# Maxima of a group set 0.13 of a head behind its turn instead of 0.07

## What is computed

```python
q = rmsnorm(x @ Wq); k = rmsnorm(x @ Wk); v = x @ Wv          # 16 heads of 64
gate = softplus(einsum('bthd,hd->bht', k, u_n) / sqrt(D))
bias = -dist[None, None] * omega_eff[None, :, None, None] * gate[:, :, None, :]
bias = where(causal[None, None], bias, -inf)
scores = einsum('bihd,bjhd->bhij', q, k) * scale + bias
attn = softmax(scores, axis=-1)
y = einsum('bhij,bjhd->bihd', attn, v).reshape(B, T, H * D)
```

## Time and profile before

| | us |
|---|---|
| median of 3 runs | 3415.65 (3412.11 to 3420.32) |
| profiled execution | 3416.66 |
| its span in the trace | 3414.9 |
| PE busy | 3174.5 (93%) |
| ACT busy | 1796.5 (53%) |
| DVE busy | 1667.0 (49%) |
| POOL busy | 1499.5 (44%) |
| L907 (PE, maxima), busy / idle before | 463.6 / 79.1 |

### The profile page before, as it was taken

The page is one execution under the profiler, slowest core; times in us unless marked ns, Lnnn a source line. Parts: engine busy times, 40 slices in busy tenths (PEclk is TensorE's granted clock), DMA queues, the critical chain, the costliest instruction groups (busy, mean ns, idle before and its releaser), DMA issues. The chain is left out here.

```text
span 3414.9 us, 45979 instructions
## 1 busy us (share of the span) xinstructions
PE 3174.5 (93%) x15472; PEld 2462.6 (72%) x15472; DVE 1667.0 (49%) x3920; ACT 1796.5 (53%) x3057; POOL 1499.5 (44%) x1318
## 2 busy tenths in 40 slices
PE   4999999999999999999999999779999999899998
PEld 3667767767667677677677676557777878688887
DVE  6566565566565665655655666242222222232322
ACT  1576676667666666666766677532222222222222
POOL 4576676666666666666765666411111110000000
PEclk7899999999999999999999999889999999899999
DMA  2232332322432422322323223343222321322120
GB/s 75 66 89 55 69 79 51 84 62 55 92 79 61 98 55 56 92 54 68 84 49 80 66 54 89 88 120 94 87 87 86 89 87 42 99 73 74 38 74 19
DMA packets 196539, 249.12 MB, mean 73 GB/s; under 512 B 67280, under 2 KB 95056, under 8 KB 196176
## 3 DMA queue, kind: packets, MB, share of 16 engines
q1 hardware_dynamic: 196304, 246.19, 28.1%
HBM read 84.86 MB, written 43.52 MB: 38 GB/s over the span
## 5 line engine op out<-in xcount | busy, mean ns | idle before, releaser
L385 POOL TENSOR_TENSOR e_lo<-e_all,e_hi 128x512 fp32r<-128x512 f32 (+1 forms) x832 | 1031.8, 1248 | 676.3 <-ACT e_all L627 618.3
L627 ACT ACTIVATE e_all<-ps_s,bias 128x512 f32<-128x512 f32 (+3 forms) x1280 | 790.6, 623 | 182.4 <-PE ps_s L929 73.1
L620 ACT ACTIVATE e_hi<-ps_s,bias 128x512 fp32r<-128x512 f32 (+1 forms) x832 | 559.5, 672 | 272.2 <-PE ps_s L927 173.3
L814 DVE TENSOR_REDUCE maxes<-ps_m 128x1 f32<-128x512 f32 x768 | 519.5, 686 | 340.6 <-PE ps_m L907 336.4
L907 PE MATMUL ps_m<-k_ext,q_max 128*128 128x512 f32 (+3 forms) x1280 | 463.6, 382 | 79.1 <-issue 30.1
L926 PE MATMUL ps_s<-q_twice,k_split 128*128 128x512 f32 (+3 forms) x1280 | 484.5, 378 | 6.1 <-ACT e_all L627 3.1
L927 PE MATMUL ps_s<-q_ext,k_ext 128*128 128x512 f32 (+3 forms) x1280 | 472.3, 369 | 0.0
L960 PE MATMUL ps_v<-e_lo,v_main 128*66 128x512 f32 (+1 forms) x832 | 432.9, 520 | 15.5 <-POOL e_lo L385 15.5
L811 DVE CUSTOM_DVE_ANT_0 ps_m<-ps_m,mask_row 128x128 f32<-128x128 f32 (+3 forms) x512 | 253.6, 497 | 363.9 <-PE ps_m L907 360.4
L907 PEld LDWEIGHTS ps_m<-k_ext,q_max 128*128 128x128 f32 x1280 | 246.9, 194 | 230.2 <-issue 81.5
L949 PE MATMUL ps_v<-e_hi,v_main 128*66 128x512 f32 (+1 forms) x832 | 324.8, 390 | 0.0
(11 more groups left out here) (247 smaller groups left out, 6120.5 us busy)
## 6 DMA issues: line engine op xcount, KB each, us to landing
q_twice<-q_max SPq DMA_DIRECT2D x256, 128.0 KB, 2.3
yt<-y_out SPq DMA_DIRECT2D x128, 130.0 KB
k_ext<-kq_hi SPq DMA_DIRECT2D x128, 128.0 KB, 2.3
q_max<-kq_hi SPq DMA_DIRECT2D x128, 128.0 KB, 2.4
k_split<-kq_hi SPq DMA_DIRECT2D x128, 128.0 KB, 2.4
k_split<-kq_lo SPq DMA_DIRECT2D x128, 128.0 KB, 2.4
q_ext<-kq_lo SPq DMA_DIRECT2D x128, 128.0 KB, 2.4
y_in<-yt SPq DMA_DIRECT2D x128, 128.0 KB, 3.0
```

The costliest lines, as they stand in the source:

```text
L385: on.tensor_tensor(e_lo[:, i % LO_RING, off:QB], e_all[:, u_ % E_RING, off:QB], e_hi[:, i % HI_RING, off:QB].bitcast(F32), ALU.subtract).t ...
L620: nc.scalar.activation(e_hi[:, i % HI_RING, off:QB], ps_s[u_ % 2][:, off:QB], ACT.Exp, bias=by).then_inc(hi_done, 1)
L627: nc.scalar.activation(e_all[:, u_ % E_RING, off:QB], ps_s[u_ % 2][:, off:QB], ACT.Exp, bias=by).then_inc(ex_done, 1)
L814: nc.vector.tensor_reduce(maxes[:, qt, kc:kc + 1], ps_m[m % 2][:, 0:width], AX.X, ALU.max).then_inc(mx_free, 1)
```

## The change

The distance at which maxima may stand behind their group's turn becomes 0.13 of a head instead of 0.07. The maxima of a pair's first head run from there to t0 + 0.24 (before: t0 + 0.20), those of the second from t0 + 0.27 (before: t0 + 0.24) to t0 + 1.08 as before.

```diff
--- before.py
+++ after.py
@@ -119,10 +119,10 @@
             turns = [first + 0.005 + 0.066 * i for i in range(NTURN)]
             for i, when in enumerate(turns):
                 at(when, "turn", n, i)
-            start, end = (turns[0] + 0.07, t0 + 0.20) if s == 0 else (t0 + 0.24, t0 + 1.08)
+            start, end = (turns[0] + 0.13, t0 + 0.24) if s == 0 else (t0 + 0.27, t0 + 1.08)
             for v, (qt, kc) in enumerate(MAXES):
                 qb = qt // TQ
-                when = max(start + (end - start) * v / (NM - 1), turns[qb] + 0.07)
+                when = max(start + (end - start) * v / (NM - 1), turns[qb] + 0.13)
                 at(when, "max", n, v)
                 if v + 1 == maxes_to(qb):
                     at(when + 0.001, "most", n, qb)
```

## The result

The changed kernel takes **3401.34 us** (median of 9 runs, 3397.03 to 3408.38) where the kernel before, on the same chip, takes 3415.65 (9 runs, 3412.11 to 3424.59): a ratio of 0.9959, 95% interval 0.9947 to 0.9971. That is faster by 14.3 us. The forecast was 3384 us, a gain of 31.5; the time lies inside the wide range (3350 to 3406), but outside the forecast's own (3370 to 3397), and more than half of the gain is missing. The profiled execution took 3401.34 us with a span of 3399.6, 15.3 us less than the one of before (3414.9), so the two traces show the whole difference.

A forecast was written before the change was run, and what follows sets the result against it. PE was taken as the bound in attention, with 84.7 us hanging on operand waits and lost clock. Terms 37.7 - 1.2 - 5 = 31.5 us gave 3384 us from 3415.65; own range 3370 to 3397, wide range 3350 to 3406.

The forecast's parts named there:

- The mechanism: First maxima wait less; ACT, before turn 3's copy into kq_hi, waits for turn 1's transfers, so PE stands 1.9 us at unit 24.
- The first rival: Turn 3's copy holds nobody up and the waits simply go: 68 us come back, 3348 us, chance 0.12.
- the fourth: Rival: the first maximum's release moves with PE's order and the stall returns in full; 3416 us, chance 0.07.
- The third: Rival: the clock falls for double length, 3.4 us, in every pair, 51 us in all; slower, 3430 us, chance 0.06.
- The second rival: The clock falls behind each new wait, 25.5 us in place of 5: a gain of 11, 3404 us, chance 0.15.
- left at the first maxima and second groups: First maxima of 15 pairs keep about 0.9 us each, 15 us in all; second groups no longer wait for q_max.
- new wait for e_all: Behind turn 3, unit 24's scores wait for e_all: 1.9 us in pair 1, about 33 us in all.
- clock still lost: Behind the new waits before unit 24, three clock falls at 1.7 us: -5 us (0 to 25).
- The step that failed first: DVE becoming the bound with maxima closer (0.81 of a head, not 0.84) was left out: busy 22.1 of 46 us.
- Unit 24: Starts 1.1 us behind the landing of turn 1's last transfer; mark to mark over 15 pairs a gain of 37.7 us.
- The first maximum: In each pair it comes 2.07 us later behind nine matmuls, the release stays at 202.1 (pair 1), about 0.9 us left.
- The start: Before the program's first scores, three maxima leave PE's idle wait for q_twice and DVE's chain comes later: -1.2 us (0.7 to 2).

The follow-up runs named there:

- the ring of three: The changed kernel with kq_hi and kq_lo as rings of three buffers in place of two (x_rows sharing sq's memory): 3361.47 us (0.9833).
- late loads: The changed kernel with the five w_in transfers issued 0.3 of a head later (t0 - 2.30 in place of t0 - 2.60): 3362.64 us (0.9841).
- the ring alone: The kernel before, distance 0.07, with kq_hi and kq_lo as rings of three buffers and x_rows in sq: 3414.76 us (0.9998).
- the shorter queue alone: The kernel before, distance 0.07, with the w_in transfers issued at t0 - 2.30 in place of t0 - 2.60: 3402.22 us (0.9957).
- with both: The changed kernel with kq_hi and kq_lo as rings of three buffers and the w_in transfers issued at t0 - 2.30: 3358.74 us (0.983).

## Why the mechanism was right and the sum was wrong

**The mechanism** was the one forecast. The first maximum no longer waits 2.9 us; turn 3's copy in ACT waits for turn 1's q_ext; unit 24 stands behind it; the second groups' first maxima wait in three places (1.8 us in all) where they waited 11.7. The first rival (nobody waits for turn 3) is refuted by the 42.7 us on ACT before turn 3's copy and by the ring of three, the fourth (nothing moves) by 1.09 in place of 2.91. The third (slower) did not come. The second rival has the nearest time, 3404, but with the clock falling behind each wait; it fell seven times. That its time comes nearest is luck. And that 3401 lies inside the range at all comes of a range drawn wide enough to take in that rival.

**The sum** failed in its sizes. In the terms of the forecast, with the trace's own numbers:

| | forecast | measured |
|---|---|---|
| left at the first maxima and second groups | 15 | 22.6 |
| new wait for e_all | 33 | 20.2 |
| more waits for DVE's maxima | 0 | 10.6 |
| more at e_lo and x_rows | 0 | 2.7 |
| clock still lost | 5 | 11.9 |

The first two together are 42.8 us, 5 below the forecast. The three others are 20 us above it; the net of 15 is nearly all of the 16.2 us that the traces lack of the forecast gain (15.3 in place of 31.5).

- **The step that failed first** is the one that left DVE out: "it is busy for 22.1 of 46 us there". The row is right, but it is a mean, and it begins 16 us behind the second head's turn 0, while the largest new wait stands 3 us behind that turn. Cutting the trace of before at the same marks gives 22.6 of 41.7, 21.8 of 41.9 and 33.2 of 45.1 us: the last part stood at 74% already. But the largest new wait, 0.68 us, stands in the part in which DVE is busy for about half of the time; there it is held by order, 1.25 us for ACT and then five operations in a row, which no share of busy time shows. A deferred maximum was priced at its matmul (0.35 us for two). The count says more: PE now runs 6, 22, 27 and 25 maxima in the four stretches of pair 1 (turn 0 to unit 24, to the second head's turn 0, to unit 24 of the first head, to the next pair), before 8, 23, 25 and 24. So three more stand behind the second head's turn 0. A typical pair gains 0.3 us between unit 24 and that turn, and then loses 0.95 and 0.26. **Over the pairs the two stretches behind the second head's turn 0 cost 15.3 us, where the forecast had 5.3 for the deferred maxima and nothing for DVE.** This is read from the traces; no run takes the waits for DVE away alone. The distance by itself (20.7 us of waits for DVE, from 100 us to the end of the attention, 9.6 before) and the ends by themselves (15.9) each bring some.
- **Unit 24** was set at the landing plus 1.1 us; it is 1.36, another 4 us over 15 pairs. Turn 1 also landed later behind turn 0 by 1.3 us in all. These two are the 5 us that are missing up to unit 24.
- **The clock** was counted at three falls of 1.7 us, and there are seven: a term of 5 us that measured 11.9. Two of them, in pairs 4 and 6, come between the first maximum and unit 24 and cost nothing there, for unit 24 waits for the transfer anyway. Four others (pairs 5, 9, 10, 11) run into the matmuls behind it, at about 1.3 us each, and the one of pair 7 stands at a wait for x_rows.
- **Pair 7** takes 3.7 us longer between unit 24 and the second head's turn 0. The waits for x_rows give 0.9 of it (3.35 and 0.63 us, where before there were 1.61, 0.59 and 0.86), the clock fall at the longer of them 1.7, and two waits for DVE's maxima 1.1. A single wait for x_rows of 2 to 3.5 us stands there in other kernels with a larger distance too (2.1 at 0.16, 3.5 with late loads), and was not in the forecast.
- **The first maximum** was to keep 0.9 us and keeps 0.77 to 2.38, 20.8 in all. The 2.07 us of the nine matmuls came off as worked out; but "the release stays" was wrong. In pairs 4, 5, 6 and 9 SP issues k_ext<-bias_rows 1.0 to 1.6 us later behind turn 0 than before, 5.0 us in all (in pair 8 it was late before as well). The rest is the way from that issue to PE's start: the prediction read 2.8 us for all pairs, the trace of before has 2.80 to 3.07, and this one 2.81 to 3.14. SP in pair 4:

```profile
585.11 2.72 SPq L427 DMA_DIRECT2D bias_rows<-bias_out  x4
```

  Issuing these four takes 2.72 us (one of them 1.40), where the same four take 1.74 in pair 1. Why, no run here shows. Its cost is small here, for unit 24 is held by turn 1's landing, which in these four pairs comes 0.2 to 0.6 us later. In the kernel with late loads, where unit 24 is seldom held, it costs more: there unit 24 starts 13.8 us behind turn 0 in pair 1, and 14.8 to 16.8 us behind it in pairs 4, 5, 6, 8 and 9 (in 5 and 9 with a clock fall).
- **The start** was set at -1.2 us; the first scores come 1.28 us later behind turn 0. From there to pair 1's turn 0 it is another 1.2. As pair 0's turn 0 itself came 0.7 us sooner in this trace, 1.8 us are left.

Run from mark to mark, the sum of 15 pairs from turn 0 to unit 24 is a gain of 37.9 us (43.0 forecast: 37.7 and 5.3 for the two deferred maxima). All the rest of the program was to give back 11.5, and gives back 22.6: 1.8 up to pair 1, 4.3 from unit 24 to the second head's turn 0, 15.3 behind it, 1.3 behind the attention. The prediction watched the place of the change closely and the remainder of the pair hardly at all.

What stays open: which of DVE's operations beside the second head's turn 0 would have to move for the 0.68 us to go, whether the ends of the maxima gain 4 to 6 us at the distance of 0.13, and why they lose 9 at 0.07; and what slows PE's steps where no wait is listed.

## What to carry to other kernels

When a stall for an operand is removed by going to it later, look for the next holder of the same chain: the buffer that the transfer reads from, the queue between two batches of transfers. Here the move alone was worth 14 us, the ring alone nothing that can be told (1 us) and the shorter queue alone 13; the move with the ring was worth 54, with the queue 53, with both 57. Work that is put off lands somewhere: count it by stretch, and read the busy share and the order of the engine that takes it in that stretch, not in the mean. And place such a constant by trial around the value (here 0.10, 0.13, 0.16): one side pays for the operand, the other mostly for the engine behind.

## What the runs showed of the hardware

**The clock.** That it may fall behind waits this short was not expected: in the trace of before the falls stood behind waits of 2.8 us and more. In the changed kernel six falls come behind waits of 1.91 to 2.07 us (the seventh at one of 3.35), and waits of 2.00, 2.04 and 2.38 us have none. Scores of unit 24 in pairs 5 and 12, and the granted clock (the last but two of the columns) in the 10 us behind each:

```profile
731.86 0.47 PE L926 MATMUL ps_s<-q_twice,k_split 128*128 128x512 f32 x1 [1.97 <-ACT e_all L627]
...
1659.83 0.47 PE L926 MATMUL ps_s<-q_twice,k_split 128*128 128x512 f32 x1 [2.04 <-ACT e_all L627]
```

```profile
733.00:743.00 10.00, 10.00 (x39) 7.08 (x39) 6.20 (x16) 7.00 (x12) 6.14 (x5) 0.83 0.61 137
...
1660.00:1670.00 10.00, 10.00 (x44) 6.86 (x44) 7.16 (x20) 7.87 (x13) 6.45 (x5) 1.00 0.68 152
```

With the distance of 0.16 the wait before unit 24 was 1.81 to 3.38 us in fourteen pairs (pair 15 has none), and a fall stood behind eleven of them; after the one of 2.45 us at 344.07 the clock shows 1.00 from 346 to 356 us, after the one of 2.43 at 212.58 it shows 0.85 from 214 to 224. In the kernel with both edits a wait of 3.48 us, at 987.81, has 1.00 behind it; at the distance of 0.10 with late loads there is a fall behind one of 1.73 us (pair 14). So between 1.7 and 3.4 us the length of a wait alone does not tell whether the clock falls. The Trainium skill (TensorE: Matmul & The Clock Gate, Part 1) says that the count runs free of the program; these rows agree, and so does the mean clock of the nine runs of the changed kernel, which goes from 0.968 to 0.974. As an estimate, falls in this band are a share of the waits: here a third (6 of the 17 waits of 1.7 to 2.4 us in the changed kernel) to three quarters (11 of 14 at 0.16), where the forecast took one in five. Single waits of 1.5 us and less had none behind them in the traces of before and after.
